# Turning three quantised weight matrices with transposing DMAs instead of with TensorE: a gated attention block on one Trainium2 core

## What is computed

```
x = x + tanh(g_xattn) * attention(layernorm(x), ctx, ctx)       # softmax over the queries, causal
n = layernorm(x)
xq   = fake_quant(n, scale = sigmoid(clip_x) * max|n| / 127)      # one maximum over the whole tensor
gate = xq @ quant(w_gate).T ;  up = xq @ quant(w_up).T            # weights: one scale per row
h    = fake_quant(silu(gate) * up, scale = sigmoid(clip_down) * max|.| / 127)
x = x + tanh(g_ffn) * (h @ quant(w_down).T)
```

## Time and profile before

| | us |
|---|---|
| median of 3 runs (lowest to highest) | 109.54 (109.43 to 109.54) |
| the profiled execution, its own time | 109.32 |
| its span, first to last instruction | 107.4 |
| PE busy | 99.9 (93%) |
| DVE busy | 81.6 (76%) |
| ACT busy | 69.6 (65%) |
| POOL busy | 44.2 (41%) |

### The profile page before, as it was taken

One profiled execution on the slowest core, in us unless ns is written; L12 is line 12 of the kernel. 1 busy time (PEld: TensorE's weight loads), 2 busy tenths in 40 slices (PEclk: granted clock), 3 DMA queues, 4 the chain that ended last, 5 costly groups with the idle time before them and its releaser, 6 DMA issues.

```text
span 107.4 us, 1812 instructions
## 1 busy us (share of the span) xinstructions
PE 99.9 (93%) x600; PEld 76.8 (71%) x600; DVE 81.6 (76%) x212; ACT 69.6 (65%) x131; POOL 44.2 (41%) x80
## 2 busy tenths in 40 slices
PE   5989999999999999999999987999999699999960
PEld 2268888988989897988988973444433398788850
DVE  0275296597899979868678978649999997869990
ACT  0422252567882817457677978889988899999800
POOL 7215035065371817343192593065578540520000
PEclk9999999999999999999999999999999999999999
DMA  3999999999001411305000000000000000005547
GB/s 28 383 384 260 386 419 422 410 406 395 31 23 26 33 16 14 38 1 57 0 0 0 0 0 0 6 0 3 0 0 0 0 6 0 0 0 195 195 148 249
DMA packets 5769, 12.18 MB, mean 113 GB/s; under 512 B 1280, under 2 KB 2048, under 8 KB 5760
## 3 DMA queue, kind: packets, MB, share of 16 engines
q1 hardware_dynamic: 5184, 11.28, 31.8%
q10 hardware_dynamic: 576, 0.79, 2.1%
HBM read 9.96 MB, written 2.10 MB: 112 GB/s over the span
## 4 chain that ended last, share of the span: by engine, by line
PE 52%; ACT 18%; DVE 17%; issue 4%; DMA 4%; ACTq 1%; DVEq 0%
PE ps L457 13%; PE ps L479 11%; PE ps L497 10%; ACT ints L890 7%; DVE shared L1124 5%; DVE hmax L1129 4%; ACT xn L801 4%; DMA wq_sb<-in_wq 4%; PE ps L650 3%; PE ps L507 3%; PE ps L509 2%; PE ps L508 2%; PE ps L554 2%; ACT silu L863 2%; PE ps L669 2%
## 5 line engine op out<-in xcount | busy, mean ns | idle before, releaser
L650 PE MATMUL ps<-xq,wguT 128*128 128x512 bf16 x80 | 17.7, 379 | 0.8 <-DVE xq L1104 0.8
L428 POOL TENSOR_TENSOR shared<-up_sb,silu 128x1024 f32<-128x1024 f32 x5 | 11.8, 2365 | 9.7 <-ACT up_sb L868 9.7
L650 PEld LDWEIGHTS ps<-xq,wguT 128*128 128x128 bf16 x80 | 7.6, 98 | 10.6 <-DVE shared L1124 1.1
L457 PE MATMUL ps<-wvT,shared 128*128 128x256 f32 x56 | 13.3, 380 | 0.0
L479 PE MATMUL ps<-shared,a_sb 128*128 128x256 f32 x56 | 13.2, 379 | 0.0
L1129 DVE TENSOR_REDUCE hmax<-shared 128x1 f32<-128x2048 f32 (+1 forms) x6 | 12.7, 2108 | 0.6
L863 ACT ACTIVATE silu<-ps,gu_scale 128x1024 f32<-128x1024 f32 x10 | 11.1, 1115 | 2.5 <-PE ps L650 2.5
L744 ACT ACTIVATE probs<-neg_scores,neg_max 128x256 f32<-128x256 f32 x8 | 4.1, 508 | 12.7 <-DVE neg_max L941 12.5
L497 PE MATMUL ps<-uT,shared 128*128 128x256 f32 (+1 forms) x64 | 11.9, 329 | 0.0
L457 PEld LDWEIGHTS ps<-wvT,shared 128*128 128x128 f32 x56 | 10.6, 190 | 1.6 <-issue 0.2
L497 PEld LDWEIGHTS ps<-uT,shared 128*128 128x128 f32 x64 | 10.7, 190 | 1.2
(11 more groups left out here) (131 smaller groups left out, 200.0 us busy)
## 6 DMA issues: line engine op xcount, KB each, us to landing
shared<-in_xc SPq DMA_DIRECT2D x6, 512.0 KB, 10.6
out<-xn SPq DMA_DIRECT2D x7, 256.0 KB, 2.0
xs<-in_x SPq DMA_DIRECT2D x3, 512.0 KB, 8.3
shared<-in_wgu SPq DMA_DIRECT2D x3, 512.0 KB, 7.7
shared<-in_xc SPq DMA_DIRECT2D x4, 256.0 KB, 6.0
wd<-in_wd SPq DMA_DIRECT2D x1, 768.0 KB, 10.2
r_wide<-spread SPq DMA_DIRECT2D x4, 128.0 KB, 4.0
wq_sb<-in_wq ACTq DMA_DIRECT2D x1, 256.0 KB, 3.9
```

Of the source, the lines that this page charges most:

```text
L428: nc.gpsimd.tensor_tensor(hid[:, 2 * i + 1, :], up_sb[i % 2][:], silu1[i % 2][:], ALU.mult).then_inc(hid_done[1], 1)
L457: last = nc.tensor.matmul(bank2(VB[b])[:, k, :], ctxT(b)[:, e, k * P:(k + 1) * P], weights[:, e, :], start=(e == 0), stop=(e == KT - 1))
L650: last = nc.tensor.matmul(bank(4 * half + 2 * g + c), wguT[:, i, g, k, :], xq[:, k, col:col + CH], start=(k == 0), stop=(k == KT - 1))
```

## The change

- The 24 gate/up turns and the 12 down turns on PE go, with the copies out of PSUM (three on ACT and DVE for gate/up, four on ACT for down) and POOL's memset.
- SP issues six transposing DMAs (128x512 bf16 each, SBUF to SBUF) for gate/up and two (128x896 bf16 each) for down, after the last reload of `r_wide` and ahead of the stores.
- PE waits for all six (`wguT_here`) ahead of the first gate/up product and for both others (`wdT_here`) ahead of the first down product.
- The host pads the down weights to 7 blocks of 128 columns, of which the last two hold the 64 left-over columns beside 64 zeros, so `wd`, `wd_i16` and `wd_q` grow from 768 to 896 columns; the maximum is still taken over 704.
- `turn_x1` starts in banks 4 and 5 instead of 6 and 7, directly behind the last gate/up product; ACT copies all eight x tiles ahead of its first quantisation; the waits of `spread_max(1, 7)` and of the down steps are adapted.

```diff
-        X1T_BANKS = (6, 7, 0, 1, 2, 3, 4, 5)
+        X1T_BANKS = (4, 5, 6, 7, 0, 1, 2, 3)
...
+            for s in range(SLOTS):
+                sp.wait_ge(wgu_q_done, s + 1)
+                sp.dma_start_transpose(wguT[:, s].rearrange("p n k i -> p (n k) i"),
+                                       wgu_q[:, s].rearrange("p n d -> p (n d)")).then_inc(wguT_here, 16)
+            sp.wait_ge(wd_q_done, 1)
+            for t in range(KT):
+                sp.dma_start_transpose(wdT[:, :, t * P:(t + 1) * P], wd_q[:, t]).then_inc(wdT_here, 16)
...
-            pe.wait_ge(vh_ready, LAST - 1)
-            turn_gate_up(0, WT)
             scores(LAST - 1)
             project_queries(LAST)
-            pe.wait_ge(wguT_ready, 1)
-            turn_gate_up(1, WT)
-            turn_gate_up(2, X2)
             scores(LAST)
             attend(LAST - 1)
...
-            pe.wait_ge(wguT_ready, 2)
-            pe.wait_ge(wguT_last, 1)
+            pe.wait_ge(wguT_here, 16 * SLOTS)
...
-            pe.wait_ge(silu_done[1], FULL)
-            turn_down(0, 4)
-            turn_down(1, 5)
...
-            pe.wait_ge(up_out_done, FULL)
+            pe.wait_ge(silu_done[1], FULL)
             turn_x1(0)
             turn_x1(1)
-            pe.wait_ge(silu_done[0], FULL + 2)
+            pe.wait_ge(up_out_done, FULL)
             turn_x1(2)
             turn_x1(3)
...
-            pe.wait_ge(x1T_ready, 2)
+            pe.wait_ge(x1T_ready, 4)
             spread_max(1, 7)
...
+            pe.wait_ge(wdT_here, 16 * KT)
...
-            wdT_out()
-            for c in range(STEPS - 2):
+            for c in range(STEPS):
                 x1T_out(c)
             act.wait_ge(act_inv_done, 2)
...
             hidden_ints(2, 0, THIRD_ACT_SLOTS)
-            for c in (STEPS - 2, STEPS - 1):
-                x1T_out(c)
...
-        "wd": np.concatenate([down, down[:, :, FULL * P:I]], axis=2),
+        "wd": np.concatenate([down, none, none, down[:, :, FULL * P:I]], axis=2),
```

More of the change, by code:

```diff
@@ L34 @@
 SLOTS = FULL + 1
+WD_BLOCKS = FULL + 2
 STEPS = NT // 2
@@ L72, in gated_block @@
         wvT_g = sb("wvT_g", [P, KT, D])
-        wd = sb("wd", [P, KT, SLOTS * P])
+        wd = sb("wd", [P, KT, WD_BLOCKS * P])
         scalars = sb("scalars", [P, 4])
@@ L125, in gated_block @@
         wdinv = sb("wdinv", [P, KT])
-        wd_i16 = sb("wd_i16", [P, KT, SLOTS * P], I16)
-        wd_q = sb("wd_q", [P, KT, SLOTS * P], BF16)
+        wd_i16 = sb("wd_i16", [P, KT, WD_BLOCKS * P], I16)
+        wd_q = sb("wd_q", [P, KT, WD_BLOCKS * P], BF16)
         wguT = sb("wguT", [P, SLOTS, 2, KT, P], BF16)
-        wdT = sb("wdT", [P, FULL, D], BF16)
-        wdT_rest = sb("wdT_rest", [P, 2, D], BF16)
+        wdT = sb("wdT", [P, WD_BLOCKS, D], BF16)
         col_max = sb("col_max", [P, 2])
@@ L256, in gated_block @@
         wd_q_done = sem("wd_q_done")
[L257 to L261, removed]
+        wguT_here = sem("wguT_here")
+        wdT_here = sem("wdT_here")
         x1_turned = sem("x1_turned")
@@ L518, in transposes2 @@
                 last.then_inc(tr2_done, 1)
[L520 to L538, removed]
             def spread_max(n, bk):
@@ L609, in _ @@
                 attn_done, 1)
-            for b in (0, 1, 2):
+            for b in (0, 1, 2, 4):
                 transposes2(b)
-            pe.wait_ge(wguT_last, 1)
-            transposes2(4)
             pe.wait_ge(x1_done, LAST)
@@ L710, in down_products @@
                             last = nc.tensor.matmul(down_half(c, t)[:, half * P:(half + 1) * P],
-                                                    wdT_rest[:, half, cols], hq[c % HQ_BUFS][:, 2 * FULL, :],
+                                                    wdT[:, FULL + half, cols], hq[c % HQ_BUFS][:, 2 * FULL, :],
                                                     start=False, stop=(half == 1))
                         last.then_inc(down_done, 1)
+            pe.wait_ge(wdT_here, 16 * KT)
             first = FIRST_SLOTS // 2
@@ L722, in _ @@
                 if c < STEPS - 1:
-                    pe.wait_ge(x1T_ready, c + 2)
+                    pe.wait_ge(x1T_ready, min(c + 4, STEPS))
                 else:
@@ L779, in quantise_down_weights @@
                     wdint_done, 1)
-            def wguT_out(n, bk):
-                act.wait_ge(wgu_tr, n + 1)
-                nc.scalar.copy(wguT[:, 2 * n:2 * n + 2].rearrange("p s n k i -> p (s n k i)"),
-                               ps[:, bk, :].bitcast(BF16)).then_inc(wguT_ready, 1)
-            def wdT_out():
-                act.wait_ge(wd_tr, 1)
-                nc.scalar.copy(wdT[:, 0:3, :].rearrange("p s h -> p (s h)"),
-                               ps[:, 4, :].bitcast(BF16)[:, 0:3 * D]).then_inc(wdT_ready, 1)
-                act.wait_ge(wd_tr, 2)
-                nc.scalar.copy(wdT[:, 3:5, :].rearrange("p s h -> p (s h)"),
-                               ps[:, 5, :].bitcast(BF16)[:, 0:2 * D]).then_inc(wdT_ready, 1)
-                act.wait_ge(rest_zeroed, 1)
-                for half in range(2):
-                    rows = slice(half * REST, (half + 1) * REST)
-                    nc.scalar.copy(wdT_rest[rows, half, :],
-                                   ps[rows, 5, :].bitcast(BF16)[:, 2 * D:3 * D]).then_inc(wdT_ready, 1)
             def x1T_out(c):
```

17 lines of the change are left out of this document (4 added, 13 removed).

## The result

| | median us (range, runs) | ratio to before, 95% interval |
|---|---|---|
| before | 109.54 (109.43 to 109.64, 4) | |
| changed kernel | 107.85 (107.63 to 108.13, 4) | 0.9847 [0.9821, 0.9874] |
| the same, timed again twice | 107.95 (5 runs), 108.17 (5 runs) | 0.9859 [0.9831, 0.9887], 0.9864 [0.9840, 0.9887] |

The account below looks back on a forecast made before the run. Chains of waits bound the kernel: PE in attention, DVE to barrier 1, DVE and ACT nearly together at barrier 2, DVE in the down stretch. 0.25 + 0 + 0 + 0.48 + 0 = 0.73 us, 109.54 to 108.8; range 108.3 to 109.5.

Parts of the forecast that it names:

- Part 1: End of attention: gate/up turns leave PE, of 1.34 us removed 0.25 us come back, through an earlier row maximum of batch 6.
- its work before that ends at 51.29 + 0.75 = 52.04: DVE ahead of the row maximum of batch 6: that maximum can move only from 52.32 to about 52.07, 0.25 us.
- The bound of 0.27: Upper bound of the gain at the end of attention: DVE's whole idle time before the row maximum of batch 6.
- Part 2: Six gate/up transposing DMAs before the first gate/up product: overlapping, there by 53.1; cost 0 to 5.8 us, value 0.
- rival 1: Gate/up transfers land late, PE waits at the first gate/up product: at 4.0 us each 5.8 us slower, 114.6 us; chance 0.17.
- Part 3: Barrier 2: down weights leave PE and ACT; of 1.96 us removed at most 0.08 show, taken as 0.
- Part 4: Down stretch: two x copies leave it, DVE's clip of step 3 starts at 95.91 instead of 96.39, gain 0.48 us.
- The bound of "0.49, the whole idle time": Upper bound of the down-stretch gain: DVE's wait for ACT's integers of step 3.
- from then on clips and finishes without idle time in a rhythm of 1.36: DVE in the down stretch after its wait for ACT's integers of step 3: no idle time, 1.36 us a step.
- The best case, 108.7: Whole kernel: 109.54 less the upper bounds 0.27, 0.08 and 0.49; with 0.4 for build differences, 108.3.
- half of the rest: Half of the chance 0.02 given to something else, such as transfers disturbing the table load or stores; counted as slower.
- Rival 3: PE loses its clock in the new 1.06 us gap before the scores of batch 7: some 113 us; chance 0.03.

Follow-up runs that it names:

- xcopies_back: The changed kernel with two of the eight x copies put back behind ACT's first four quantisations: 108.51 us, ratio 0.9918 to the kernel before.
- down_first: The changed kernel with the two down-weight transfers issued ahead of the six of gate/up on SP: 113.54 us, ratio 1.0354 to the kernel before.

## Why the prediction was right and wrong

- **Part 1 (0.25 forecast, 0.35 measured).** Mechanism right: 0.99 of the removed 1.34 us were cover for a wait on DVE, and PE stood idle for them. The step that was mis-sized is "its work before that ends at 51.29 + 0.75 = 52.04": the next instruction started, in the changed kernel, 0.67 us after the pair (52.49 - 51.82), not 0.75. The bound of 0.27, "DVE's whole idle time", fell for the same reason: idle time in a timeline begins only where the row before it ends, and that is later than the engine could have gone on.
- **Part 2 (0 forecast, 0 measured).** Right; rival 1 is refuted for this place in the queue. The price of an issue was not: 1.27 us on SP instead of 0.32, so the six were there at 57.7 instead of 53.1. By the Trainium skill's figure (VectorE: DVE Perf Modes, "The three transpose paths", 1309 ns a block) 24 blocks one by one would have taken 31.4 us, an estimate from that page; the traces have 1.31 us from one issue to the next for four blocks, and 9.1 us (`down_first`) to 9.7 us (the changed kernel) from the first issue to the last landing. By the Trainium skill's other rule (Advanced Engine Details and Errata, "X-Bar Transpose (TRN2)", as fast as regular DMAs) the traces don't agree either: 125 GB/s while only they run, against up to 423 for the loads.
- **Part 3 (0 at the barrier).** Right: -0.70 on one side of barrier 2 and -0.71 on the other, ACT waiting 0.75 us.
- **Part 4 (0.48 forecast, 0.57 and another 0.20 measured).** The place was right, `xcopies_back` shows it. Two steps failed. The bound of "0.49, the whole idle time" failed as in part 1. And "from then on clips and finishes without idle time in a rhythm of 1.36" took the pace of ACT for that of DVE: the `finish` pairs of the kernel before start 0.91 us ahead of the next clip (96.84 to 97.75), those of the changed kernel 0.79 (96.08 to 96.87), and the 0.12 us between was a wait for ACT that doesn't show, because the row before it ends late. The chain of the kernel before names ACT for that stretch; I took the timeline of DVE instead. The prediction had "DVE's step rhythm no longer 1.36" among its signs of being wrong, and that sign came: 1.22. With the copies gone ACT leads, DVE catches up, and PE with 1.32 us a step sets the end, which I had as the next in line: its last product moved by 0.27 us from barrier 2 on, and since DVE's last `finish` had stood in a queue, it moved by 0.57. SP's queue of stores, which I had not costed, gave 0.20: its last issue came 0.23 us after the end of the last `finish` before, and 0.03 after it now. The 0.03 stands in every kernel with the moved copies and the DMAs; in the kernels whose down stretch is as before, or without one of the two, it is 0.10 to 0.29, so this share is 0.1 to 0.3 us.
- **What the sum didn't have: DVE's second product (0.33 us).** I wrote that the diff leaves the gate/up stretch alone, and didn't ask why its chain holds 0.41 us of "issue". The diff takes one DVE instruction away ahead of it, and that was enough.
- **The range.** The best case, 108.7 with 0.4 below it, was built from the same two bounds. 0.35 + 0.33 + 0.57 + 0.20 = 1.45 us, 108.1, is what the traces carry, already below the range. Of the 0.72 us that the sum of 0.73 lacked, the missing term has 0.33, the stores 0.20, and the two mis-sized bounds 0.10 and 0.09. The rest, up to the 1.69 of the first comparison, is within the spread of runs: 1.41 to 1.69 in three comparisons. One sum of the chances is off: rivals 1 and 3 and half of the rest make 0.17 + 0.03 + 0.01 = 0.21, not 0.19; nothing hangs on it.
- **Rival 3.** A gap of 0.99 us on PE left the clock full; one of 4.29 us did not.

## What to carry over

Before taking "no idle time" on an engine for its pace, look at the start-to-start distances and at whom the chain of waits names there: rows reach past the start of the next instruction, and short waits vanish in that. Idle time on a timeline is then no upper bound of what an earlier input brings. In the down half of this change, the work moved to the DMA queue paid by the room that it made for other work at a barrier: the four copies removed brought nothing until two others were shifted into their place. And a few tenths of "issue" in the chain of a short kernel are worth one idle instruction as a test, ahead of any theory on the change itself.

## What the runs showed of the hardware

- One instruction's place in DVE's stream can cost 0.41 us when DVE comes to it from a wait: one memset more at the start of the kernel before made it 0.7% faster (0.9928 [0.9902, 0.9955]), of which its trace places 0.34 us. An 8 KB packet of kind `instruction` is tied to the same place, 1.1 us later. A boundary between blocks of instructions is likely; how it holds DVE is open.
- Transposing DMAs of 128x512 bf16 from SBUF to SBUF cost SP 1.27 us of issue each, land in 2.5 us in `down_first`, where they follow nothing but other transposing DMAs (3.7 us as a median beside the last reload), are moved in packets under 512 B (6400 in the whole run against 1280 before), and show 125 GB/s.
- TensorE turned the same 24 blocks in 1.34 us, 56 ns each, while it was running anyway.
- After 4.3 us idle PE's granted clock was still 1.00 for the first 0.7 us of work and then 0.50 from 69.9 to 73.3; after 0.99 us idle it stayed at 1.00.
- A row of DVE reaches past the start of the next instruction: 0.75 us long, with the next start 0.67 us after its own.
